# A fused transformer layer on one core: the attention's probabilities are transposed by 32x32 squares and transfers instead of by TensorE

## What is computed

```
x = x + 0.5 * ffn(layernorm(x))
x = x + attention(layernorm(x))
x = x + 0.5 * ffn(layernorm(x))

attention(x):                       # one head, 4096 memory slots, width 128
    q = x @ Wq.T + bq
    scores = q @ memory_keys.T / sqrt(128)          # 4096 x 4096
    probs = softmax(scores)
    return (probs @ memory_values) @ Wo.T + bo

ffn(x):                             # 8 experts of width 176, the two best per token
    s = sigmoid(x @ gate_w.T); the two experts with the highest s + expert_bias
    routed: relu(s_e * x @ w_up[e].T)^2 @ w_down[e].T, in bfloat16, summed over both
    shared: relu(x @ shared_up.T)^2 @ shared_down.T
```

## Time and profile before

| | |
|---|---|
| time, median of 3 runs | 715.12 us (714.81 to 717.83) |
| the profiled execution | 713.79 us, span 712.0 us |
| instructions | 10456 |
| PE / DVE / ACT / POOL busy | 675.9 / 549.5 / 474.0 / 121.9 us |
| transfers | 4327 packets, 10.87 MB |

### The profile page before, as it was taken

One profiled execution on the slowest core, in us unless ns is written; L12 is line 12 of the kernel. 1 busy time (PEld: TensorE's weight loads), 2 busy tenths in 40 slices (PEclk: granted clock), 3 DMA queues, 4 the chain that ended last, 5 costly groups with the idle time before them and its releaser, 6 DMA issues.

```text
span 712.0 us, 10456 instructions
## 1 busy us (share of the span) xinstructions
PE 675.9 (95%) x3521; PEld 503.8 (71%) x3536; DVE 549.5 (77%) x1176; ACT 474.0 (67%) x893; POOL 121.9 (17%) x226
## 2 busy tenths in 40 slices
PE   3898988999999999999999999999999999989997
PEld 3444444788888888888888888888888888745542
DVE  3799876877876886787688677778867875799885
ACT  3577887757666756756666675666666665478886
POOL 4755412102000200200020020002001021242200
PEclk9899999999999999999999999999999999999999
DMA  7011100000000000000000000000000000000001
GB/s 279 2 46 44 59 30 0 1 1 0 1 2 1 1 0 1 1 1 1 0 1 1 1 0 1 1 1 1 0 1 1 1 1 0 1 1 30 31 16 44
DMA packets 4327, 10.87 MB, mean 15 GB/s; under 512 B 859, under 2 KB 1459, under 8 KB 4147
## 3 DMA queue, kind: packets, MB, share of 16 engines
q1 hardware_dynamic: 3987, 10.21, 4.2%
q10 hardware_dynamic: 288, 0.01, 0.0%
HBM read 8.12 MB, written 2.10 MB: 14 GB/s over the span
## 4 chain that ended last, share of the span: by engine, by line
PE 82%; DVE 8%; issue 4%; ACT 4%; POOL 1%; DMA 0%; ACTq 0%; DVEq 0%; POOLq 0%
PE banks L1088 15%; PE banks L1111 8%; PE banks L1110 8%; PE banks L1112 8%; PE banks L1073 8%; PE banks L1074 8%; PE banks L1075 8%; PE banks L953 4%; PE banks L962 3%; DVE probs L697 3%; PE banks L969 2%; PE banks L1120 2%; PE banks L909 2%; ACT probs L435 1%; PE banks L901 1%
## 5 line engine op out<-in xcount | busy, mean ns | idle before, releaser
L542 ACT ACTIVATE p_hi<-banks 128x512 fp32r<-128x512 f32 x256 | 154.0, 602 | 134.4 <-PE banks L1088 134.2
L784 DVE TENSOR_TENSOR p_lo<-banks,p_hi 128x512 fp32r<-128x512 f32 x256 | 176.2, 689 | 82.6 <-ACT p_hi L542 80.7
L821 DVE TENSOR_REDUCE bank_max<-banks 128x1 f32<-128x512 f32 x256 | 171.0, 686 | 30.2 <-PE banks L1075 26.4
L553 ACT ACTIVATE probs<-banks,neg_max 128x512 f32<-128x512 f32 (+1 forms) x192 | 158.8, 833 | 14.7 <-DVE neg_max L842 14.7
L1088 PE MATMUL banks<-ident,probs 128*128 128x128 f32 x1024 | 153.4, 272 | 1.4 <-DVE p_lo L784 1.4
L1088 PEld LDWEIGHTS banks<-ident,probs 128*128 128x128 f32 x1024 | 126.2, 140 | 36.5 <-issue 5.1
L1110 PE MATMUL banks<-p_hi,kv_lo 128*128 128x512 f32 x256 | 120.0, 469 | 0.6 <-DVE p_lo L784 0.6
L446 ACT ACTIVATE probs<-probs 128x1024 bf16<-128x1024 bf16 x96 | 92.1, 979 | 33.1 <-DVE probs L697 24.3
L697 DVE SCALAR_TENSOR_TENSOR probs<-banks,wbc 128x1024 bf16<-128x1024 f32 x80 | 95.4, 1218 | 22.5 <-PE banks L953 19.5
L1073 PE MATMUL banks<-kv_lo,q_parts 128*128 128x512 f32 x256 | 102.6, 401 | 1.2 <-issue 1.2
L1111 PE MATMUL banks<-p_lo,kv_hi 128*128 128x512 f32 x256 | 101.4, 396 | 0.0
(11 more groups left out here) (87 smaller groups left out, 708.4 us busy)
## 6 DMA issues: line engine op xcount, KB each, us to landing
kv_stage<-in_keys_values SPq DMA_DIRECT2D x8, 512.0 KB, 3.5
out<-X SPq DMA_DIRECT2D x8, 256.0 KB, 2.0
X<-in_x SPq DMA_DIRECT2D x1, 1280.0 KB, 9.2
X<-in_x SPq DMA_DIRECT2D x3, 256.0 KB, 5.3
probs<-in_wup SPq DMA_DIRECT2D x1, 704.0 KB, 5.2
probs<-in_wdown SPq DMA_DIRECT2D x1, 704.0 KB, 6.6
sup_s<-in_shared_up SPq DMA_DIRECT2D x1, 88.0 KB
sdown_s<-in_shared_down SPq DMA_DIRECT2D x1, 88.0 KB
```

The source lines that it names most:

```text
L542: act.activation(p_hi[:, c % 4, :], TB[c % 2][:, :], ACT.Copy).then_inc(p_hi_done, 1)
L553: act.activation(probs[:, v % 2, i, first * N:(first + count) * N], score_banks(u, i)[:, first:first + count, :].rearrange("p b n -> p (b ...
L784: dve.tensor_tensor(p_lo[:, c % 4, :], TB[c % 2][:, :], p_hi[:, c % 4, :].bitcast(fp32), ALU.subtract).then_inc(p_lo_done, 1)
L821: dve.tensor_reduce(bank_max[:, i % 2, q:q + 1], score_banks(u, i)[:, q, :], AX.X, ALU.max).then_inc(bank_max_done, 1)
```

## The change

Only the attention and what feeds it is changed.

- TensorE's transposes are gone. The exponentials go to `E2`, a ring of two tiles. VectorE transposes each half tile (128 x 1024) in place by squares of 32x32 (`transpose_squares`). SP then issues 16 transfers per tile, each 32 partitions x 512 values from `E2` to `probsT`, which put the squares where slots are on the partitions. The keys are handed over in an order that makes the chunks come out whole.
- `probsT` is a ring of two units. `p_hi` and `p_lo` are made for pairs of chunks, 128 x 1024 from SBUF, in a ring of three. Of four pairs VectorE subtracts one (L842) and GpSimd three (L400); after the last scores VectorE takes two in three.
- The maximum goes over two banks at once. Scores use a ring of six banks. The values of a chunk come 26 score banks behind (`LAG`).
- The loops run by tile (S) instead of by unit; `project_out` and the additions move to fixed places in them. The early transposes and gates of the second feed-forward use the y and z banks; `xT`, `xTb` and `wbc` lie in `E2`'s memory.

```
+LAG = 26
+SQ = 32
+QUADS = P // SQ
+SCORE_BANKS = 6
+HI_RING = 3
...
+        def on_vector(m):
+
+            return m % 4 == 1 or (2 * m + LAG > LAST_SCORE_SLOT and m % 3 != 0)
...
+            for S in range(SCORE_TILES):
+                u, t = divmod(S, GT)
+                if S == 0:
+                    sp.wait_ge(z_done, GROUPS)
+                    sp.wait_ge(down_done, GROUPS * SLOTS)
...
+                if t == 0 and u >= 2:
+                    wait_split(sp, (u - 1) * KC // 2 - 1)
+                for h in range(2):
+                    sp.wait_ge(squares_done, 2 * S + h + 1)
+                    for b in (2 * h, 2 * h + 1):
+                        for i in range(QUADS):
+                            sp.dma_start(probsT[b * SQ:(b + 1) * SQ, u % 2, t * QUADS + i, :, :],
+                                         E2[i * SQ:(i + 1) * SQ, S % 2, b, :].rearrange("p (c q) -> p c q", q=SQ)
+                                         ).then_inc(moved[S % 2], 16)
...
+            def p_low(m):
+
+                pool.wait_ge(p_hi_done, m + 1)
+                pool.tensor_tensor(p_lo[:, m % HI_RING, :, :], pair_probs(m), p_hi[:, m % HI_RING, :, :].bitcast(fp32),
+                                   ALU.subtract).then_inc(p_lo_done, 1)
...
+            def p_high(m):
+
+                w, c = divmod(2 * m, KC)
+                if c == 0:
+                    act.wait_ge(moved[0], unit_moves(w))
+                    act.wait_ge(moved[1], unit_moves(w))
+                wait(act, pv_done, 2 * (m - HI_RING + 1))
+                act.activation(p_hi[:, m % HI_RING, :, :], pair_probs(m), ACT.Copy).then_inc(p_hi_done, 1)
...
+                    wait(act, moved[S % 2], 16 * QUADS * QUADS * (S // 2))
...
+            def attention():
+                for S in range(SCORE_TILES + LAG // BANKS + 2):
+                    u, i = divmod(S, GT)
+                    first, second = 2 * S - 11, 2 * S - 10
+                    if 0 <= first < VALUE_PAIRS:
+                        p_high(first)
+                    if 1 <= S <= SCORE_TILES:
+                        exponentials(S - 1, 0)
+                        exponentials(S - 1, 1)
...
+                    if 0 <= second < VALUE_PAIRS:
+                        p_high(second)
+                    if 1 <= S <= SCORE_TILES:
+                        exponentials(S - 1, 2)
...
+            def transpose_squares(S, h):
+
+                dve.wait_ge(exp_done, S * len(EXP_PIECES) + 2 + h)
+                part_of = E2[:, S % 2, 2 * h:2 * h + 2, :].rearrange("p b n -> p (b n)")
+                dve.transpose(part_of, part_of).then_inc(squares_done, 1)
+
+            def attention():
+                for S in range(SCORE_TILES + LAG // BANKS + 2):
+                    u, i = divmod(S, GT)
+                    if 1 <= S <= SCORE_TILES:
+                        maximum(S - 1, 1)
+                        negative_maximum(S - 1)
+                    if 0 <= 2 * S - 11 < VALUE_PAIRS and on_vector(2 * S - 11):
+                        p_low(2 * S - 11)
...
+                    if S < SCORE_TILES:
+                        maximum(S, 0)
...
+                    if 1 <= S <= SCORE_TILES:
+                        transpose_squares(S - 1, 0)
+                        transpose_squares(S - 1, 1)
...
-                for t in range(GT):
-                    last = pe.transpose(TB[c % 2][:, t * P:(t + 1) * P],
-                                        probs[:, (v + 1) % 2, t, c * P:(c + 1) * P], ident[:, :])
-                last.then_inc(probsT_done, 1)
...
+            def attention():
+                for n in range(LAST_SCORE_SLOT + LAG):
+                    S, q = divmod(n, BANKS)
+                    u, at_slot = divmod(n, KC)
+                    if 2 <= n < LAST_SCORE_SLOT:
+                        scores(S, q)
...
+                    if n >= LAG:
+                        values(*divmod(n - LAG, KC))
```

More of the change, by code:

```diff
@@ L196, in macaron_kernel @@
         exp_done = sem("exp_done")
-        probsT_done = sem("probsT_done")
+        squares_done = sem("squares_done")
+        moved = [sem(f"moved{b}") for b in range(2)]
         p_hi_done = sem("p_hi_done")
         p_lo_done = sem("p_lo_done")
+        p_lo_tail_done = sem("p_lo_tail_done")
         pv_done = sem("pv_done")
@@ L229, in wide_weights, with score_bank, pair_probs, splits_up_to @@
             return early_wide if G // 2 == GROUPS // 2 else weight_wide
[L231 to L237, removed]
+        def score_bank(S, q):
+            return (S * BANKS + q) % SCORE_BANKS
+        def pair_probs(m):
+            w, c = divmod(2 * m, KC)
+            return probsT[:, w % 2, :, c:c + 2, :].rearrange("p a c q -> p a (c q)")
+        def on_vector(m):
+            return m % 4 == 1 or (2 * m + LAG > LAST_SCORE_SLOT and m % 3 != 0)
+        def splits_up_to(m, vector):
+            return sum(1 for k in range(m + 1) if on_vector(k) == vector)
+        def wait_split(eng, m):
+            eng.wait_ge(p_lo_tail_done if on_vector(m) else p_lo_done, splits_up_to(m, on_vector(m)))
+        def unit_moves(w):
+            return 16 * QUADS * QUADS * (GT // 2) * (w + 1)
         def tiles_of(g):
             return bass.ds(g * GT, GT)
[L242 to L252, removed]
         @block.sync
@@ L395, in _ @@
+            attention()
             ffn(1)
@@ new lines, in add_second_block, with maximum @@
+            def add_second_block(g):
+                dve.wait_ge(out_proj_done, 2 * g + 2)
+                dve.wait_ge(first_block_added, g + 1)
+                for t in range(GT):
+                    last = dve.scalar_tensor_tensor(
+                        X[:, g * GT + t, :], OB[1][:, t * D:(t + 1) * D], share[:, 1, t:t + 1],
+                        X[:, g * GT + t, :], ALU.mult, ALU.add)
+                last.then_inc(x_attended, 1)
+            def maximum(S, h):
+                dve.wait_ge(scores_done, S * BANKS + 2 * h + 2)
+                at_bank = score_bank(S, 2 * h)
+                dve.tensor_reduce(bank_max[:, S % 2, h:h + 1],
+                                  banks[:, at_bank:at_bank + 2, :].rearrange("p b n -> p (b n)"), AX.X, ALU.max
+                                  ).then_inc(bank_max_done, 1)
```

549 lines of the change are left out of this document (244 added, 305 removed).

## The result

| | before | after |
|---|---|---|
| median | 715.5 us (714.8 to 717.8, 4 runs) | **911.8 us** (909.6 to 912.4, 4 runs) |
| ratio after/before | | **1.273** [1.270, 1.277] |
| profiled execution, span | 713.8, 712.0 us | 911.7, 909.9 us |
| mean granted clock of TensorE | 0.995 | 0.859 |

The forecast was 735 us, 668 to 755. The sign was right and the size was not: 177 us are missing, and the range misses them too.

A forecast was written before the change was run, and what follows sets the result against it. TensorE, 95% busy, bounded the kernel; SyncE's issues would next: 127.7 us start + 481.3 issues + 15 x 1.0 idle, last values product at 642.0, + 91.3 = 733.3 span, + 1.8 around it: 735 us, range 668 to 755.

The forecast's parts named there:

- What the transfers add: SyncE's 64 transfers per attention unit: 0.47 us per issue whatever the size, 30.1 us per unit on SyncE alone.
- start of the first transfer: Attention start: first maximum at 119.85 us, then products, maxima, exponentials and square transposes, so SyncE starts at 127.7 us.
- SP's idle time and longer issues: SyncE once per attention unit: waiting for the next squares, 1.0 us each, 15 times; longer issues were not forecast.
- last issue to the last product of values: Attention end: landing, splitting, a GpSimd subtraction of 2.35 us, sixteen chunks of values in 13 us; last product at 642.0.
- the hold: ScalarE's first splitting per unit waits for all 64 transfers, delaying the next squares; SyncE idles 1.0 us per unit (0.5 to 2.5).
- bound of 0.49: SyncE's upper issue distance, from 6.41 us over 13 issues: 31.4 us per unit, setting the range's high end of 755.
- That SP is the bound: Attention after the change: SyncE's issuing comes last, 31.1 us per unit with its wait; every other engine needs less than 30.1.
- The moving: DMA engines: 0.17 us per transfer, 11 us per unit, hidden behind 0.47 us issues; DMA share about 0.25 to 0.35.
- The hidden prices: Other engines' attention work, hidden behind SyncE: two-bank maximum and square transpose 1.13 us each on VectorE, GpSimd subtraction 2.35 us.
- rival D: VectorE's square transposes cost double, 33.2 us per unit on VectorE: 769 us; chance 0.05.
- rival E: TensorE's products slow down with 32-element pieces as moving operand, needing 0.32 instead of 0.233 us: not likely, still 735 us.
- Rival B: SyncE issues cost 0.37 us, the tile cycle bounds, 28.0 us per unit: 685 us; wins below 0.445 per issue; chance 0.30.

The follow-up runs named there:

- experiment 1: Kernel with only rows of 24 transfers, layer left out, run once: SyncE issues last 0.589 to 0.616 us from SBUF to SBUF, 0.421 for 32 rows from DRAM.
- wide4: Changed kernel with 4 transfers of 128 partitions per tile in place of 16 of 32, same bytes, wrong values: 667.5 us, 0.931 of the kernel before.
- after_r: Changed kernel with only ScalarE's second splitting moved behind the tile's third exponential: 909.7 us, 1.271 of the kernel before.
- wide8: Changed kernel with 8 transfers of 64 partitions per tile in place of 16 of 32, wrong values: 710.8 us, 0.992 of the kernel before.
- 11/5/0: Changed kernel, SyncE issuing 11 of a tile's 16 transfers, GpSimd 5, ScalarE none, ScalarE's second splitting behind the third exponential: 745.3 us, 1.042 of the kernel before.

## Why the prediction was wrong in size

**The step that failed is the price of one issue**, the 0.47 us of "What the transfers add"; it measured 0.633. Forecast and profile, term by term:

| term | forecast | trace after |
|---|---|---|
| start of the first transfer | 127.7 | 129.5 |
| 1024 issues at 0.47, at 0.633 | 481.3 | 648 |
| SP's idle time and longer issues | 15.0 | 15 |
| last issue to the last product of values | 18.0 | 25 |
| from there to the end of the span | 91.3 | 92.4 |
| span | 733.3 | 909.9 |

1024 x (0.633 - 0.47) = 167 of the 177 us; the other 10 are 2 at the start, 7 behind the last issue and 1 at the end. The 15 of idle time agree by luck: the forecast meant the hold, and in the profile SP's waits are 5.6 us, and the rest is some longer issues (up to 1.84 us) whose cause no run shows. The distance was read from loads out of DRAM, the only row of issues in the trace, and the transfers of the change go from SBUF to SBUF. The prediction asked if size matters (from SBUF to SBUF it hardly does, 0.589 to 0.616; 128 rows from DRAM do get dearer in a row, where the DMA engines are full) and if an issue after a wait is short (right: 0.507 against 0.590 in experiment 1). Isolated issues were fourteen and not eight, six loads and eight stores, all alike; none went from SBUF to SBUF. It never asked if the pair of source and destination matters, though all rows it had were of other pairs. Its bound of 0.49 came from the same rows, so the range was too narrow upward: it was the spread of one kind of issue, not the uncertainty about another.

**That SP is the bound: right.** SP's 5.6 us of waits in 663 say it, and wide4 shows it with the same bytes. The Trainium skill's sentence that the time to start a DMA is usually small relative to the DMA itself (DMA: Bandwidth & Descriptors, "Issuing engines are not separate DMA queues") doesn't hold here: 0.64 us against 0.41 x 0.64 = 0.27 us of the 16 engines' time, and against 2.0 us from issue to landing it is a third.

**The moving: hidden, as said, but dearer.** 0.27 us per transfer and not 0.17; share 0.41 against a forecast of 0.25 to 0.35. Here the pair of memories is not the reason: wide4 moves 158 GB/s from SBUF to SBUF at the same share of 0.41. Its transfers have 128 rows as the stores have, and a packet of 2 KB takes a median of 84 ns in it and 86 in the stores; in the change, with 32 rows, it takes 142. The price was read from transfers of 128 rows; the error had no effect on the time.

**The hold of ScalarE: there, but SP hardly idled.** Forecast 1.0 us per unit, measured 5.6 / 16 = 0.35. Eight issues of the next half tile take 5.1 us at the true price, longer than the 4.9 until the next squares are done, so the dearer issue covered it: after the hold shown above, those squares end at 424.31 and SP starts on them at 424.48, without a pause. after_r bears that out: the order changes nothing.

**The hidden prices: right.** Maxima over two banks and square transposes in a row start 1.13 to 1.17 us apart (1.20 and 1.24 us busy, not the 2.3 of rival D), GpSimd's subtraction takes 2.39 (2.35), VectorE's 1.24. TensorE's products are no slower with 32-element pieces: 0.24 apart at full clock (rival E out).

**TensorE's clock was not in the forecast.** Before, TensorE was busy without a break and had full clock. Now it waits for exponentials 49 times, 4.1 us on average, and the granted clock is 0.85 in the stretch above. While SP is last it can cost little, 5.6 us at most by SP's waits; behind the last issue it may be part of the 7 us. wide4, with TensorE at 93%, has 1.00.

**Rival B was the right picture of a kernel with cheap issues**: wide4 has a unit in (579.0 - 184.8) / 15 = 26.3 us from projection to projection, B had 26.2 without and 28.0 with the hold; 667.5 us against 685. But its condition, 0.445 us per issue, was never near.

## What to carry to other kernels

In these runs a transfer cost its issuing engine a time that hardly depended on its size while the DMA engines had room, and did depend on the memories at its ends: count issues per unit of work first, and take the price from an issue of the same kind or measure it, since a row of the wrong kind gives no bound. When work is moved to small transfers, the sum to make is issues x price per engine against the present time per unit; here 64 x 0.64 = 41 us against 30 says no before anything else is considered. When a bound engine was relieved here by sharing its work, the helpers' queues, their order and the engine that they lock out took its place.

## What was not expected of the hardware

- An issue from SyncE takes 0.59 to 0.60 us from SBUF to SBUF, for 16 to 64 rows and 128 B or 2 KB alike, and 0.42 for 32 rows from DRAM (experiment 1). ScalarE 0.61 and GpSimd 0.50 from SBUF to SBUF. After a wait it is 0.51 from SBUF to SBUF, and 0.33 both for loads and for stores. Why the pair matters, no run shows.
- A packet of 2 KB from SBUF to SBUF took a median of 142 ns in transfers of 32 rows (change), 149 with 64 (wide8), 84 with 128 (wide4); 86 in the stores, of 128 rows. So wide8 holds the DMA engines at 0.64 where wide4 holds them at 0.41, with no more bytes.
- VectorE's subtraction of two SBUF tiles goes from 1.2 to 4.7 us behind two GpSimd subtractions, while its maximum and its squares don't change. Order alone can bring it on: in after_r the mean is 1901 ns instead of 1238, with no effect on the time, as SP is last.
- The same hits a tiny instruction: VectorE's minimum of two SBUF tiles over 128x4 values took 0.15 us before and up to 4.35 us in 11/5/0.
